# Two pairs of turned heads exchange their PSUM homes in an attention kernel on one core

## The reference

```python
scores = jnp.einsum('bhid,bhjd->bhij', q * scale, k)      # 16 heads, 256 x 256
probs = jax.nn.softmax(scores, axis=-1)
attn = jnp.einsum('bhij,bhjd->bihd', probs, v)            # v: a mixture of 8 experts per head
...
x = x + 0.5 * _L0_ffn_ref(_layernorm(x, axis=-1), ...)
x = x + _L0_attn_ref(_layernorm(x, axis=-1), ...)
x = x + 0.5 * _L0_ffn_ref(_layernorm(x, axis=-1), ...)
```

## Time and profile before

| | us |
|---|---|
| median of 3 runs | 2558.63 (2554.79 to 2559.12) |
| profiled execution, its own time | 2555.17 |
| its span | 2553.4 |
| TensorE busy / weight loads busy | 2469.9 / 2321.9 |
| ScalarE busy | 2073.2 |
| VectorE busy | 1983.8 |
| GpSimd busy | 1138.9 |

### The profile page before, as it was taken

The page is one execution under the profiler, slowest core; times in us unless marked ns, Lnnn a source line. Parts: engine busy times, 40 slices in busy tenths (PEclk is TensorE's granted clock), DMA queues, the critical chain, the costliest instruction groups (busy, mean ns, idle before and its releaser), DMA issues.

```text
span 2553.4 us, 111659 instructions
## 1 busy us (share of the span) xinstructions
PE 2469.9 (97%) x45824; PEld 2321.9 (91%) x45824; DVE 1983.8 (78%) x3498; ACT 2073.2 (81%) x6373; POOL 1138.9 (45%) x1126
## 2 busy tenths in 40 slices
PE   4999999999999999999999999999999999999997
PEld 3899999999999999999999999999999999999997
DVE  4787777778877778888788787788787788887874
ACT  3888888888888888888888888888888888888885
POOL 2354545445445345344445354454453453444431
PEclk8999999999999999999999999999999999999998
DMA  4555555655656656555555556556556556556553
GB/s 130 149 154 147 144 146 140 163 151 153 162 147 158 158 152 157 146 164 148 157 159 155 155 150 166 149 154 164 146 155 158 153 157 157 152 145 156 162 155 99
DMA packets 519351, 387.58 MB, mean 152 GB/s; under 512 B 214080, under 2 KB 436160, under 8 KB 510656
## 3 DMA queue, kind: packets, MB, share of 16 engines
q1 hardware_dynamic: 518416, 379.60, 55.5%
q10 hardware_dynamic: 432, 0.85, 0.1%
HBM read 191.64 MB, written 188.74 MB: 149 GB/s over the span
## 4 chain that ended last, share of the span: by engine, by line
PE 80%; ACT 10%; issue 5%; DVE 3%; POOL 1%; DMA 1%; SPq 0%; ACTq 0%; DVEq 0%; POOLq 0%
PE psT L451 16%; PE psS L408 15%; PE psS L490 7%; PE psT L490 7%; ACT PB L758 7%; PE psT L468 6%; PE psT L470 5%; PE psT L469 5%; PE psT L463 5%; PE psT L421 5%; PE psT L435 4%; DVE NMAX L639 2%; ACT PT L846 1%; ACT QK L767 1%; DVE QK L698 1%
## 5 line engine op out<-in xcount | busy, mean ns | idle before, releaser
L758 ACT ACTIVATE PB<-psS,NMAX 128x256 f32<-128x256 f32 x2048 | 943.5, 488 | 246.5 <-DVE NMAX L639 246.5
L451 PE MATMUL psT<-V,PT 128*64 128x64 f32 x16384 | 540.4, 224 | 7.3 <-issue 7.1
L451 PEld LDWEIGHTS psT<-V,PT 128*64 128x64 f32 x16384 | 502.4, 138 | 35.1 <-issue 10.0
L698 DVE TENSOR_TENSOR QK<-psT,QK 128x512 fp32r<-128x512 f32 x512 | 341.1, 688 | 211.4 <-ACT QK L767 209.3
L639 DVE TENSOR_REDUCE NMAX<-psS 128x2 f32<-128x512 f32 x512 | 329.6, 685 | 202.9 <-PE psS L408 202.4
L758 ACT ACTIVATION_READ_ACCUMULATOR PB<-psS,NMAX 128x1 f32 x2048 | 452.6, 221 | 0.0
L408 PE MATMUL psS<-QK 64*128 64x256 f32 x6144 | 434.7, 286 | 14.8 <-ACT PT L846 13.1
L408 PEld LDWEIGHTS psS<-QK 64*128 64x128 f32 x6144 | 389.6, 186 | 63.5 <-issue 63.3
L767 ACT ACTIVATE QK<-psT 128x512 fp32r<-128x512 f32 x512 | 298.7, 622 | 84.1 <-PE psT L470 69.4
L864 POOL TENSOR_TENSOR BT<-MT,diagv 128x1024 f32<-128x1024 f32 x128 | 308.4, 2410 | 118.0 <-DMA MT<-MIXd 118.0
L641 DVE TENSOR_REDUCE NMAX<-psS 128x4 f32<-128x1024 f32 x256 | 310.9, 1214 | 0.0
(11 more groups left out here) (119 smaller groups left out, 4582.2 us busy)
## 6 DMA issues: line engine op xcount, KB each, us to landing
Vd<-VM SPq DMA_DIRECT2D x128, 512.0 KB, 3.9
V<-Vd SPq DMA_DIRECT2D x128, 512.0 KB, 5.2
AOd<-AO SPq DMA_DIRECT2D x256, 256.0 KB, 3.7
PJd<-PJ SPq DMA_DIRECT2D x64, 512.0 KB, 2.6
PR<-PJd SPq DMA_DIRECT2D x64, 512.0 KB, 4.0
MIXd<-MIX SPq DMA_DIRECT2D x64, 128.0 KB, 2.0
MT<-MIXd SPq DMA_DIRECT2D x64, 128.0 KB, 4.5
MASKd<-MASKR SPq DMA_DIRECT2D x64, 128.0 KB, 3.6
```

The source lines that it names most:

```text
L451: last = eng.matmul(M[64 * u:64 * u + 64, (t * NT + it) * DH:(t * NT + it + 1) * DH], PT[:, t, jt, cols], V[:, pm % 2, 4 * r + t, jt, :], ...
L698: eng.tensor_tensor(QK[:, 1, ab], bank("qk", m).rearrange("p (k t) -> p k t", k=2), QK[:, 0, ab].bitcast(F32), ALU.subtract).then_inc(free ...
L758: eng.activation(PB[:, ab, j, it, :], psS[:, ab, j, it, :], ACT.Exp, bias=NMAX[:, ab, j, it:it + 1], accum_out=SUM[:, p % 2, it, 4 * r + t ...
```

## The change

The homes of the turned heads are exchanged. Before, t = 0 and 1 go to `psS[:, 0]` and t = 2 and 3 to the ring; now t = 0 and 1 go to the ring and t = 2 and 3 to `psS[:, 1]`, the banks of their own pair's scores. The order of the turns and of the copies stays. Thus the copies that the scores wait for are others: the first pair's scores wait for no copy, the second pair's wait for those of t = 2 and 3. The ring has as many items as before, at the same places.

```diff
             if works(n):
-                items += [("turn", n, t) for t in (2, 3)]
+                items += [("turn", n, t) for t in (0, 1)]
...
         def turned(n, t):
 
-            return psS[:, 0, t].rearrange("p n t -> p (n t)") if t < 2 else bank("turn", n, t)
+            return bank("turn", n, t) if t < 2 else psS[:, 1, t - 2].rearrange("p n t -> p (n t)")
 
         def wait_turned(eng, n, t):
             if t < 2:
-                eng.wait_ge(s_turned, 2 * n + t + 1)
+                wait_full(eng, "turn", n, t)
             else:
-                wait_full(eng, "turn", n, t)
+                eng.wait_ge(s_turned, 2 * n + t - 1)
...
         def wait_copied(eng, n, t):
             if t < 2:
-                eng.wait_ge(s_copied[t], n + 1)
+                wait_freed(eng, "turn", n, t)
             else:
-                wait_freed(eng, "turn", n, t)
+                eng.wait_ge(s_copied[t - 2], n + 1)
...
                 if n >= 1:
                     eng.wait_ge(s_exp, 8 * (n - 1) + 4 * ab + 4)
-                if n >= 1 and ab == 0:
-                    wait_copied(eng, n - 1, 0)
-                    wait_copied(eng, n - 1, 1)
+                if n >= 1 and ab == 1:
+                    wait_copied(eng, n - 1, 2)
+                    wait_copied(eng, n - 1, 3)
...
             def turn(n, t):
                 ab, j = divmod(t, 2)
-                if t >= 2:
+                if t < 2:
                     wait_vacant(eng, "turn", n, t)
```

More of the change, by code:

```diff
@@ L253, in turned @@
         def turned(n, t):
-            return psS[:, 0, t].rearrange("p n t -> p (n t)") if t < 2 else bank("turn", n, t)
+            return bank("turn", n, t) if t < 2 else psS[:, 1, t - 2].rearrange("p n t -> p (n t)")
         def wait_turned(eng, n, t):
             if t < 2:
-                eng.wait_ge(s_turned, 2 * n + t + 1)
+                wait_full(eng, "turn", n, t)
             else:
-                wait_full(eng, "turn", n, t)
+                eng.wait_ge(s_turned, 2 * n + t - 1)
         def was_turned(n, t):
-            return s_turned if t < 2 else full("turn", n, t)
+            return full("turn", n, t) if t < 2 else s_turned
         def was_copied(n, t):
-            return s_copied[t] if t < 2 else freed("turn", n, t)
+            return freed("turn", n, t) if t < 2 else s_copied[t - 2]
         def wait_copied(eng, n, t):
             if t < 2:
-                eng.wait_ge(s_copied[t], n + 1)
+                wait_freed(eng, "turn", n, t)
             else:
-                wait_freed(eng, "turn", n, t)
+                eng.wait_ge(s_copied[t - 2], n + 1)
         def wait_x(eng, p):
```

## The result

The changed kernel takes 2623.1 us in the median of 5 runs (2621.64 to 2628.28) against 2558.63 (2553.87 to 2559.88): a ratio of 1.0262, 95% interval 1.0246 to 1.0277. The forecast was 2626, slower. The profiled execution took 2623.1 with a span of 2621.3, 67.9 more than before. The granted TensorE clock is 0.995 of full speed over it, against 0.993, so the clock has no part in the change.

What follows compares the result with a forecast made beforehand. TensorE, busy for 97% of the span, was taken as the bound; 68.9 - 8.4 - 12.2 + 20.0 = +68 us on the profiled 2555.17 gave 2623, or 2626 for the median; own range 2612 to 2640, whole range 2596 to 2652.

Steps and rivals of the forecast that it cites:

- Step 1: First pair's scores lose their copy wait: start up to 0.12 us earlier, worth nothing for TensorE.
- Step 2: Second pair's scores wait for the fourth copy: 0.27 us per quarter, +68.9 us, less 8.4 and 12.2.
- the 8.4: TensorE's existing wait for VectorE before L546 absorbs the delay in 31 quarters: -8.4 us.
- the late handovers: Handovers with copies late by ScalarE, 26 in the middle part: ScalarE becomes on time, -12.2 us.
- Step 3: First pair's turns need a ring bank 0.87 us earlier and wait for VectorE's L698: +20.0 us.
- The relief: Before the turns, TensorE's delay and earlier exponentials shrink the ring-bank waits by 0.30 or 0.25 us.
- A: At the turns, ring-bank waits get no relief: 19.5 us more, 2646 us; chance 0.15.
- B: Turns' banks cost nothing and second pair's restart is free: 2586 us, or 2606 if only banks; chance 0.14.
- C: Fourth copy done before the first pair's scores are issued, hiding all copying: 31 us gained, 2528 us; chance 0.06.
- D: TensorE's waits absorb the 0.27 us per quarter, so nothing changes: 2559 us; chance 0.05.
- the new wait: Before L408, TensorE waits for L846 between 12th and 13th matmul, some 0.2 us in nearly every quarter.
- the turns wait: L490 into psT newly waits for L698 in two of eight quarters, 0.2 to 0.4 us.

Runs made afterwards that it cites:

- second pair's wait, equal code: Kernel before, second pair's scores also waiting for the fourth copy, implied waits left out so no instruction is added: 2629.82 us, ratio 1.0282.
- ring's wait, equal code: Kernel before, turns of heads 0 and 1 waiting for the ring banks instead of those of heads 2 and 3, as many instructions: 2588.79 us, ratio 1.0122.
- both, equal code: Kernel before with the second pair's wait for the fourth copy and the ring's wait for heads 0 and 1, same number of instructions: 2648.14 us, ratio 1.0347.
- first pair waits too: Changed kernel with its own homes, first pair's scores also waiting for the copies of heads 0 and 1, equal number of instructions: 2642.89 us, ratio 1.0327.
- one shift: Kernel before with 64 identity transpositions at TensorE's start, moving its later code by 128 instructions: 2558.03 us, ratio 0.9999.
- fastest kernel: Kernel before with heads 0 and 1 moved to the second pair's psS banks, whose scores then wait for their copies: 2520.6 us, ratio 0.9854.

## Why the prediction was right

The time came out 3 us below the forecast, and the mechanisms of steps 2 and 3 stand in the trace with their numbers. But the sum was right partly by luck, because terms were off to opposite sides. By kernels of equal code it is +71 (second pair's wait), +30 (ring's banks), -12 (both together less than their sum), -25 (first pair's wait gone, with the homes): +64. This sum comes out by construction, as the last two terms are differences between the same runs.

Where the time lies can be read from the starts of all matmuls in the traces, here summed over 255 quarters and set against before, in us:

| stretch of a quarter | forecast | changed kernel | second pair's wait, equal code | ring's wait, equal code | both, equal code | first pair waits too |
|---|---|---|---|---|---|---|
| mark to the last score | +56.7 | +46.2 | +61.2 | -16.4 | +46.6 | +46.8 |
| inside the product | 0 | -3.9 | +19.3 | +2.6 | +14.3 | +14.7 |
| product's end to the first turn | +3.3 | +8.9 | -2.4 | +22.9 | +13.4 | +7.6 |
| first turn to the third | +8.3 | +17.4 | -0.1 | +24.9 | +18.3 | +18.5 |
| all | +68.3 | +69.1 | +78.1 | +33.9 | +93.2 | +87.4 |

The forecast's column is the prediction's own terms put at their places; "all" has the small rest of a quarter too. These are the profiled executions, whose times lie up to 4 us beside the medians.

*Step 1, the first pair's scores.* "For TensorE it is worth nothing" holds for the scores themselves: they start at the mark + 0.20, so leaving the transpositions takes 0.20 by itself, and the copy had held them for 0.03 where it was on time, and for 0.09 in three kinds of quarter of eight. For the kernel it failed. With the wait TensorE's stops in the product go too, from 19.0 us to 5.9 of idle time, and it is worth 20 to 25 us instead of 0.

*Step 2, the second pair's scores.* In five kinds of quarter of eight the last score comes 0.26 later, in two 0.20, and in the late one 0.24 earlier; the term came out 10 us smaller than forecast. L546 gave 7 of the 8.4. The wait alone was forecast at 68.9 - 8.4 - 12.2 = 48 and measured 71. There the late handovers do not gain: "with TensorE later, ScalarE is on time there" holds only when the turns wait as well. With the second pair's wait alone (of equal code) the timeline there reads

```profile
1341.37 1.04 PE L491 MATMUL psT<-ident,PB 128*128 128x128 f32 x8
1341.42 1.08 ACT L847 ACTIVATE PT<-psS 128x512 f32<-128x512 f32 x2
...
1342.38 1.11 ACT L847 ACTIVATE PT<-psT 128x512 f32<-128x512 f32 x2
...
1342.65 1.96 PE L409 MATMUL psS<-QK 64*128 64x256 f32 x24 [0.24 <-ACT PT L847]
```

so the mark is 1342.14 and the last score starts at 1342.65 + 1.96 - 0.28 = 1344.33, 2.19 after it, 0.10 later than before instead of 0.20 earlier: 26 x 0.30 = 8 us. The products take another 19 us, which no term of the prediction has.

*Step 3, the ring's banks.* Unrelieved 30 measured and 30 expected. In the changed kernel the two kinds of quarter that the prediction charged with 20.0 us cost 19.4: the turns begin 7.3 us later in sum and the second heads and what follows them take 12.1. Quarters of other kinds add 5.3 between the first and the third turn, which the prediction had put at nothing or left to the slack at L546. The relief, 19.5 in the prediction, is 12 by the times of the kernels of equal code, where the first pair still waits; in the table the two rows of the turns are 14 below the sum of the two waits apart.

*The rivals.* A (no relief) is out, as 2648 lies 11 us below 2558 + 101. B (free banks and a free restart) is out: the ring's wait alone costs 30, and the second twelve scores take 0.70 to their last start where they took 0.64. C (faster) needed the fourth copy at the mark + 0.88; it ends at + 1.06 as before. The rule that C drew from the Trainium skill ("Perfetto Trace Analysis", section "Matmuls"), that matmul groups should rotate through PSUM banks, is borne out once the order fits: the two kernels whose first-copied heads lie in the second pair's banks gain 35 and 38 us, and the change, with the same set of banks and the last-copied heads there, loses 64. D is out. Of the signs that I gave, two were off: the new wait is not in TensorE's idle time before L408 (11.0 us), but in its busy time, and the turns wait in three kinds of quarter of eight, not in two.

## What stays open

Why TensorE stops more often in the product when both pairs wait for copies. What the traces show: at one such stop in the run with the second pair's wait alone, of equal code,

```profile
854.71 1.27 PE L452 MATMUL psT<-V,PT 128*64 128x64 f32 x36
...
856.69 1.04 PE L452 MATMUL psT<-V,PT 128*64 128x64 f32 x28 [0.71 <-issue]
```

and the transfers of 853.8 to 855.3 hold one packet of instructions:

```profile
q8 instruction: 1, 0.02, 5.5%
```

It starts 1.87 us before the edge of the block, and TensorE goes on 2.80 after its start. In that trace TensorE stops at 42 of 367 edges for more than 0.45 us; 41 of these stops end 2.2 to 2.9 us after the start of the block's packet, and it crosses no other edge sooner than 2.2 after it (median 5.5; the 42nd is the first edge of all, which has no such packet). The traces before and after show the same bound, 2.3. So at these stops TensorE waits for its code, and the product, 128 instructions in 2 us, is where it is felt most. What makes a packet start late was not tried; neither the code's place (one shift, no effect) nor its length (3 to 6, 12 and 27 us for 255, 512 and 767 instructions) explains the 19 us that hang on the first pair's wait.

The fastest kernel's profiled execution is 32 us shorter than that of before: the last scores come 28.7 us earlier (some 16 at the 37 late handovers and 13 from the others' 0.03 to 0.09), and the products take 5.2 less. The medians are 38 us apart; the other 6 us lie in the spread of the runs around the two profiled ones.

## What to carry to other kernels

When a buffer's home decides who waits for whom, give each buffer the home whose next writer comes after its copy is done. Here the first-copied heads belong in the second pair's banks, and the last-copied in the ring; the first pair's banks, which are written again soonest, stay free. Cost a moved wait at its new place by two times: when the releasing copy lets the waiter go (here the mark + 1.07 + 0.14), and when the waiter would come anyway (the mark + 0.23 + 0.79). And test the parts apart, and look where in a quarter the time lies, even if the sum comes out: the added wait alone cost 71 us where 48 were forecast, and some 19 us of it lay in the products, which that wait does not touch.

## What the runs showed of the hardware

 - A pause of TensorE of up to 0.28 us leaves no idle time in the profile: some 0.2 us per quarter raised the busy time of L408 by 63 us and its mean from 286 to 294 ns.
 - Going from the 128-row transpositions to the 64-row scores takes 0.20 us from the last start to the next with nothing to wait for (all 255 quarters of the changed kernel), where 0.11 is the pace.
 - TensorE's code comes in packets of 16 KB, 256 instructions each (94145 instructions, 367 packets). In no trace did TensorE cross a block's edge sooner than 2.1 us after the start of the block's packet, and the stops at the edges end 2.2 to 2.9 us after it (41 in the run with the second pair's wait alone at equal code). Between kernels with the same number of instructions these stops inside the product, 2.7 to 20.6 us of idle time in runs of 2520 to 2650 us, depended on which waits TensorE has.
